# Soft MoE weights split to halves in other phases, and in other pieces and queues

## What is computed

```python
x = x + tanh(g_xattn[0]) * L0_xattn(ctx, ctx, layernorm(x), ssm_kernel, D)   # causal convolution of products of 8 x 8 heads
x = x + tanh(g_ffn[0])   * L0_ffn(layernorm(x), ...)                         # 8 experts, top 2, and a shared expert
x = x + tanh(g_xattn[1]) * L1_xattn(layernorm(x), ctx, Wq, Wg, bg, Wkv, Wo)  # linear attention
x = x + tanh(g_ffn[1])   * L1_ffn(layernorm(x), gamma, beta, mu, scale, W1, b1, W2, b2)   # Soft MoE
```

```python
x_n = l2norm(x_ln) * scale;  mu_n = l2norm(mu, axis=0)
logits = einsum('bnd,des->bnes', x_n, mu_n)
dispatch, combine = softmax over tokens, softmax over all slots
slot_in = einsum('bnd,bnes->besd', x_ln, dispatch)
h = gelu(slot_in @ W1[e] + b1[e]);  slot_out = h @ W2[e] + b2[e]
out = einsum('bsd,bns->bnd', slot_out, combine)
```

## Time and profile before

| | us |
|---|---|
| median of 3 runs | 1921.96 (1918.27 to 1922.52) |
| the profiled execution | 1921.54 |
| span of its profile | 1919.8 |
| PE busy / DVE / ACT / POOL | 1594.0 / 1134.1 / 735.5 / 480.1 |

### The profile page before, as it was taken

The page is one execution under the profiler, slowest core; times in us unless marked ns, Lnnn a source line. Parts: engine busy times, 40 slices in busy tenths (PEclk is TensorE's granted clock), DMA queues, the critical chain, the costliest instruction groups (busy, mean ns, idle before and its releaser), DMA issues. The chain is left out here.

```text
span 1919.8 us, 27754 instructions
## 1 busy us (share of the span) xinstructions
PE 1594.0 (83%) x9596; PEld 927.9 (48%) x9596; DVE 1134.1 (59%) x2222; ACT 735.5 (38%) x1380; POOL 480.1 (25%) x368
## 2 busy tenths in 40 slices
PE   2978874899926988985879887586999999999997
PEld 2767762344413555552435444243555555555554
DVE  4978864555362222225768685566667676676664
ACT  2322112334321222213423332165656566565552
POOL 1334330444342433323232321134020110201000
PEclk9999996999967999996999999798999999999999
DMA  8323334333346555635330300643415143151432
GB/s 184 82 84 106 126 108 140 115 114 127 104 142 132 123 150 146 152 107 197 99 110 12 100 3 20 234 134 83 86 42 116 33 87 81 44 115 33 77 73 49
DMA packets 261179, 195.26 MB, mean 102 GB/s; under 512 B 183426, under 2 KB 212098, under 8 KB 259410
## 3 DMA queue, kind: packets, MB, share of 16 engines
q1 hardware_dynamic: 253920, 174.03, 33.6%
q0 software_dynamic: 5680, 18.62, 3.5%
q10 hardware_dynamic: 1474, 1.21, 0.3%
HBM read 110.37 MB, written 39.67 MB: 78 GB/s over the span
## 5 line engine op out<-in xcount | busy, mean ns | idle before, releaser
L1958 POOL TENSOR_TENSOR s_h_lo<-s_h,s_h_hi 128x512 f16<-128x512 f32 x32 | 37.0, 1155 | 515.9 <-DVE s_h_hi L2176 515.9
L1180 DVE TENSOR_TENSOR e_h<-e_up,e_silu 128x352 f32<-128x352 f32 x39 | 20.5, 525 | 177.7 <-ACT e_silu L1142 177.7
L507 PE MATMUL ring<-prod_hi,toep 128*128 128x288 f16 x320 | 92.8, 290 | 32.6 <-DVE terms L427 21.6
L2194 PE MATMUL s_ring<-w_mu,s_xt_hi 128*128 128x512 f16 x256 | 98.4, 384 | 15.1 <-DVE s_xt_lo L2095 14.7
L306 POOL TENSOR_TENSOR prod_lo<-prod,prod_hi 128x2304 f16<-128x2304 f32 x16 | 73.3, 4581 | 102.5 <-ACT prod_hi L343 97.8
L2195 PE MATMUL s_ring<-w_mu,s_xt_hi 128*128 128x512 f16 x256 | 98.1, 383 | 0.0
L2196 PE MATMUL s_ring<-w_mu,s_xt_lo 128*128 128x512 f16 x256 | 98.0, 383 | 0.0
L2100 DVE TENSOR_REDUCE s_top<-s_lg 128x1 f32<-128x512 f32 x64 | 43.9, 686 | 90.5 <-ACT s_lg L2004 90.3
L2194 PE MATMUL s_acc<-w_w_hi,s_g_hi 128*128 128x512 f16 x256 | 97.1, 379 | 0.2
L2194 PE MATMUL s_ring<-w_w,s_xt_hi 128*128 128x512 f16 x256 | 97.0, 379 | 0.0
L2195 PE MATMUL s_ring<-w_w,s_xt_hi 128*128 128x512 f16 x256 | 97.0, 379 | 0.0
(11 more groups left out here) (386 smaller groups left out, 4750.4 us busy)
## 6 DMA issues: line engine op xcount, KB each, us to landing
expert_rows<-e_y SPq DMA_DIRECT2D x39, 256.0 KB, 2.3
toep<-ssm_split SPq DMA_DIRECT2D x14, 512.0 KB, 5.8
stage<-in_L_ffn_gate_w SPq DMA_DIRECT2D x8, 704.0 KB
stage<-in_L_ffn_up_w SPq DMA_DIRECT2D x8, 704.0 KB
c_rows<-in_ctx SPq DMA_DIRECT2D x8, 512.0 KB, 10.2
x_rows<-in_x SPq DMA_DIRECT2D x8, 512.0 KB
res<-in_x SPq DMA_DIRECT2D x128, 32.0 KB
w_in<-in_L_ffn_W SPq DMA_DIRECT2D x16, 256.0 KB, 5.2
```

The lines of the kernel that those rows point to most:

```text
L507: nc.tensor.matmul(out, w_hi, hi, start=(n == 0), stop=False)
L2194: mm(out_, a[0], b_[0], start=first, stop=False)
```

## The change

- **Convolution.** W1 and W2 are both split there: 32 pieces (`part_in`, `part_q`, three buffers as before), two in each step on ACT and on POOL. The pieces of W2 are written to a new tensor `w2_split` in the device's memory. SP stores and reloads the pieces ahead of the step's row stores; the residual rows from the third step's on are loaded by ACT, eight transfers at the end of a step's body.
- **Experts.** `mu` goes in pieces of 256 KB, 16 loads and 16 stores, one of each with a tile; the parts of a quarter are shifted (`quarter_at`, a quarter every 8 tiles from tile 4), each engine at its own distance; the store of a tile's result is issued five tiles behind instead of three.
- **Soft MoE.** The operations `Q` are gone; W2's halves are loaded from `w2_split`, four transfers of 1 MB behind W1's. `E(3)` moves up before the last `Z`, and `E(4)` to `E(7)` of the first batch come after its first GELU in a list of their own (`body0`).

The diff, cut to its core:

```diff
@@ conv_stage
+        def load_res(eng, s):
+            for j in range(SSM_I):
+                eng.dma_start(res[j * 16:j * 16 + 16, s % 2, :], x_s[s, j]).then_inc(res_loaded[s % 2], 16)
...
+            def load_part(n):
+                v = n % PART_BUFS
+                if n < STEPS:
+                    sp.dma_start(part_in[:, v, :].rearrange("p (e h) -> p e h", e=JE), w1_d[n // KD, n % KD]).then_inc(part_loaded[v], 16)
+                else:
+                    sp.dma_start(part_in[:, v, :], w2[n - STEPS]).then_inc(part_loaded[v], 16)
...
             for s in range(STEPS):
                 if s + T_BUFS < STEPS:
                     load_toeplitz(s + T_BUFS)
                 if s == 0:
-                    for v in range(W1_BUFS):
-                        load_w1(v)
+                    for n in range(PART_BUFS):
+                        load_part(n)
+                for n in (2 * s, 2 * s + 1):
+                    store_part(n)
+                    if n + PART_BUFS < 2 * STEPS:
+                        load_part(n + PART_BUFS)
                 store(s)
-                if s + 2 < STEPS:
-                    load_res(s + 2)
-                if s >= 2:
-                    store_w1(s - 2)
-                    if s - 2 + W1_BUFS < STEPS:
-                        load_w1(s - 2 + W1_BUFS)
...
@@ conv_stage, gpsimd
                 if s >= 2:
-                    rest_of_w1(s - 2)
+                    rest_of_parts(s - 2)
@@ conv_stage, scalar
                 if s + 2 < STEPS:
                     split(s + 2)
-                split_w1(s)
+                split_parts(s)
+                if s >= 1 and s + 1 < STEPS:
+                    act.wait_ge(added, s)
+                    load_res(act, s + 1)
@@ expert_phase
-        PEEL, SPAN = 9, 9
+        PEEL, FIRST, PERIOD = 9, 4, 8
...
+        def quarter_at(n, part):
+            j, rest = divmod(n - FIRST - part, PERIOD)
+            return j if not rest and 0 <= j < NJ else None
...
@@ expert_phase, sync
+            LAG = 5
...
+            def background(n):
+                if 1 <= n <= 2 * KD:
+                    load_mu(*divmod(n - 1, KD))
+                for j, c in ((quarter_at(n, 13 + c), c) for c in range(KD)):
+                    if j is not None:
+                        store_mu(j, c)
+                        if j + 2 < NJ:
+                            load_mu(j + 2, c)
...
-                if n >= 3:
-                    store(n - 3)
...
+                if n >= LAG:
+                    store(n - LAG)
+                background(n)
@@ soft_moe_phase
-                  + softmax_in(2) + w2_split(0, 2) + E(0) + late("Z", 4) + softmax_in(3) + w2_split(2, 4) + E(1) + late("Z", 5) + softmax_in(4)
-                  + w2_split(4, 6) + E(2) + late("Z", 6) + softmax_in(5) + w2_split(6, 8) + late("Z", 7) + softmax_in(6) + softmax_in(7) + softmax_in(8)
-                  + w2_split(8, 10) + softmax_in(9) + E(3) + w2_split(10, 12) + softmax_in(10) + E(4) + w2_split(12, 14) + E(5) + w2_split(14, 16)
-                  + E(6) + E(7))
+                  + softmax_in(2) + E(0) + late("Z", 4) + softmax_in(3) + E(1) + late("Z", 5) + softmax_in(4)
+                  + E(2) + late("Z", 6) + softmax_in(5) + E(3) + late("Z", 7) + softmax_in(6) + softmax_in(7) + softmax_in(8) + softmax_in(9) + softmax_in(10))
...
+        body0 = []
+        for op in body:
+            body0 += [op]
+            if op == (0, "HG", 0):
+                body0 += E0(4) + E0(5) + E0(6) + E0(7)
...
+            for j in range(NJ):
+                sp.dma_start(w.w2[:, j].rearrange("p q e d -> p (q e d)"), w2_split[j]).then_inc(w2_in[j], 16)
```

More of the change, by code:

```diff
@@ L259, in _ @@
                     load(t, 0, u)
-            load_res(0)
-            load_res(1)
+            for s in range(2):
+                load_res(sp, s)
             for u in range(2):
@@ L1068, in _ @@
                                              ).then_inc(gathered[n % U], 16)
-                if n >= U and n - U < NJ * SPAN:
-                    quarter(*divmod(n - U, SPAN))
+                background(n)
+            for n in range(TILES, FIRST + PERIOD * (NJ - 1) + 16):
+                background(n)
         @block.tensor
@@ L1115, in step, with background @@
                     last.then_inc(contracted, 1)
-            def quarter(j, part):
-                if part == 2:
+            def background(n):
+                j = quarter_at(n, 4)
+                if j is not None:
                     pe.wait_ge(MU["ones"], 1)
@@ L1124, in quarter @@
                     last.then_inc(MU["summed"], 1)
-                if part == 4:
+                j = quarter_at(n, 6)
+                if j is not None:
                     pe.wait_ge(MU["inverted"], j + 1)
@@ L1163, in quarter @@
                     nc.scalar.activation(mu_scale[:, :], mu_ps[:, :], ACT.Copy).then_inc(MU["scale"], 1)
-                if part in (6, 7):
-                    if part == 6:
-                        act.wait_ge(MU["stored"], j * 16)
-                    for c in range((part - 6) * 2, (part - 6) * 2 + 2):
+                for j, c in ((quarter_at(n, 9 + c // 2), c) for c in range(KD)):
+                    if j is not None:
+                        if not c:
+                            act.wait_ge(MU["stored"], j * KD * 16)
                         act.wait_ge(MU["scaled"], j * KD + c + 1)
                         nc.scalar.activation(mu_q[:, 0, c, :], mu_in[:, j % 2, c, :], ACT.Copy).then_inc(MU["hi"], 1)
-            over_tiles(step, quarter)
+            over_tiles(step, background)
         @block.vector
@@ L1193, in step, with background @@
                     nc.vector.tensor_copy(y[:, u, :], out_ps[:, b, :]).then_inc(y_done, 1)
-            def quarter(j, part):
-                if part == 3:
+            def background(n):
+                j = quarter_at(n, 5)
+                if j is not None:
                     inv = mu_inv[:, j, :]
```

187 lines of the change are left out of this document (77 added, 110 removed).

## The result

| | before | after |
|---|---|---|
| median of the runs, us | 1920.12 (4 runs) | 1902.13 (1901.38 to 1905.24, 4 runs) |
| the profiled execution | 1921.54 | 1905.24 |
| its span | 1919.8 | 1903.5 |
| mean granted clock | 0.939 | 0.936 |

The ratio is 0.9913, with a 95% interval of 0.9888 to 0.9938: 18 us faster. The forecast was 1869 us, with a range from 1853 to 1889; the time lies outside it. Two of the three parts brought what was worked out for them, and the third, the convolution, lost where it should have gained.

The account below looks back on a forecast made before the run. The prediction took SP's late issuing to bind the convolution, and PE's waits for transposed rows to cost the experts. Gains of 23, 24 and 6 us (convolution, experts, Soft MoE) made 53 us: 1869 us, range 1853 to 1889.

Parts of the forecast that it names:

- the loop over two steps: Convolution: stores, SP's issuing and landing take 27.0 us, 13.5 a step; with less issuing 20.4 us, no longer binding.
- The nine waits: Convolution: PE's once-a-step waits of 19.4 us in all shrink to 0.2 us each, gaining 17.6 us.
- PE's own work: Convolution: PE's step without its wait of 2.2 us is 11.3 us; the forecast took 11.5 us a step.
- ACT's put wait: Convolution: PE's 3.39 us wait for ACT, held behind a late piece of W1, goes away, gaining 3.4 us.
- Steps 2 and 3: Convolution: the second POOL piece falls into the normalisation, where PE waits for DVE, costing 1.5 us.
- The tail: End of the convolution: row stores, not stores of W1's halves, are SP's last issues and end earlier, gaining 3.5 us.
- Rival 3: Convolution: ACT becomes the bound if an issue there costs about 1.6 us instead of 0.65; slower, chance 0.04.
- rival 1: Convolution: the DVE-POOL lock becomes the bound, each `pairs` waiting out two pieces; 7 us gained, 1880 us, chance 0.18.
- Rival 5: Convolution: SP's lateness is not the cause, so only experts and Soft MoE gain; 1892 us, chance 0.05.
- Experts: Experts: PE's waits for transposed rows mostly go and the clock rises; 24.0 us gained in sum.
- rival 2: Experts: small `mu` pieces cost as much as large ones, so the gain is 8 us, not 24; 1885 us, chance 0.08.
- Soft MoE: Soft MoE: less work on ACT and POOL brings `G` 8.1 us earlier, less 2 for the clock; 6 us gained.

Follow-up runs that it names:

- e3: The kernel after with the residual row loads back on SP's queue behind the row stores: 1903.3 us.
- e4: The kernel after with each residual load of 16 rows cut into two of 8 rows: 1868.2 us.
- e2: The kernel before with only the residual row loads moved from SP's queue to ACT's: 1937.2 us.
- e5: The kernel before with residual loads on ACT's queue and each cut into two of 8 rows: 1912.6 us.
- e1: The kernel before with only the experts' part of the change: 1895.8 us.
- e10: The kernel after with the four pairs E(4) to E(7) put back ahead of the second batch's X in the Soft MoE: 1905.6 us.
- e7: The kernel after, storing the rows of steps 0 to 13 a second time from ACT's queue in eight 32 KB transfers of 16 rows a step: 1960.4 us.

## Why the prediction was wrong

**The step that failed** is the loop over two steps of the convolution, "9.0 us to the stores, 11.5 us of issuing, 6.5 us to land". It closed to 27.0 us by the numbers, and two steps took 27.0, so I took the 6.5 us of landing for a constant and the issuing for what binds. The landing time was itself a queue behind the row transfers on two engines. When the issuing was shortened, the landing rose from 6.2 to 13.0 us. The agreement of the sum was no evidence: any loop that waits for itself closes. The DMA share of 0.37 in the earlier trace rows looked far from full; it is a mean over 16 engines, of which two had no gap: there were never fewer than two packets in flight.

Term by term:
- *The nine waits, +17.6 us.* They lost 8 us instead, 1.0 us a step. Two busy engines, with 32 KB more in each step, ask for 1.3. W2's pieces, which the prediction costed at nothing for DMA, are by that count what loads them, though no run has them alone; moving the residual rows relieves nothing, as e3 shows.
- *PE's own work, 11.3 us a step.* Right: 11.28 us in e4's shortest steps. The 11.5 us a step of the forecast was met within 0.3 us in e4 (11.8), once the rows had more engines.
- *ACT's put wait, +3.4.* It is gone, and step 5 starts 0.3 us earlier than in before (132.99, 133.25). Steps 5 and 6 then lose 3.0 us, and step 7 starts at 162.51 instead of 159.73.
- *Steps 2 and 3, -1.5.* They take 42.6 us instead of 39.4. In e4, which has the cut, it is 42.6 too, so the two engines are not the cause; nor is the second piece shown to be, since e2, which has one piece a step, takes 42.3. This stays open.
- *The tail, +3.5.* From the start of step 15 to `x_in` it is 28.2 us instead of 27.3. ACT waits 8.54 and 5.94 us there for the last pieces of W2, and the last row stores go out behind them:

```profile
280.00 0.63 ACT L352 ACTIVATE part_q<-part_in 128x512 f16<-128x512 f32 x1 [8.54 <-DMA part_in<-in_L_ffn_W]
...
291.89 0.63 ACT L352 ACTIVATE part_q<-part_in 128x512 f16<-128x512 f32 x1 [5.94 <-DMA part_in<-in_L_ffn_W]
...
295.09 4.97 SPq L245 DMA_DIRECT2D after_conv<-gated  x8
306.50 0.38 SPq L617 DMA_DIRECT2D x_in<-after_conv  x1
```

- *ACT's issues.* 0.64 us each, eight in 5.1 us, as SP's row had said. Rival 3, the slower one, was priced on the wrong thing: in e2 the move alone is slower by 17 us, at near this price of an issue (5.6 to 6.2 us for eight), and VectorE waits for loads that ACT reaches late.
- *The lock, rival 1.* It is real, but did not arise: in after `pairs` takes 2.29 and 0.42 us in the mean from 157 to 265 us, and does not meet the pieces. In e5 it costs VectorE 1.8 us a step.
- *Rival 5* came nearest: the moved work does not shorten what binds. It stood at 1892 us with a chance of 0.05, and it still had the convolution at no change. Its chance rested on the closed loop, and was too small.
- *Experts, +24.0.* 24 us by e1's median, 27 in the profile. Of PE's waits for `e_xt` only the first, 13.4 us at the phase's start, is left, and before has it too (13.1, ahead of the window of the earlier trace rows). That the small pieces would cost as much (rival 2) did not come: 256 KB pieces are no worse here than 1 MB ones, although the rule of the Trainium skill (DMA: Bandwidth & Descriptors, section "Bandwidth") that the prediction named asks for 1 MiB or more. How the gain divides was wrong: rival 2 is what happens at a store distance of 3, and at 5 it is covered, for 17.5 to 21 us and not 10. That leaves 3 to 10 us to the pieces, not the 12.3 of the two long waits.
- *Soft MoE, +6.* 5.4 us. `G` comes 91.2 us into the phase instead of 99.7, 8.5 us earlier (8.1 forecast), behind a wait of 8.18 us (6). e10 confirms that the order of the pairs is not what gave it. That leaves W2's halves, gone from ACT and POOL, which no run has alone.

The range failed as well. The lower bounds that the prediction gave its terms add up to 17 us (convolution 5 + 0 - 2.3 + 2.2, experts 12 + 0 - 1.5, Soft MoE 2), not to the 35 from which it drew its edge of 1887; the measured 18 us lie there.

With e4's cut the whole change gives 1868.2 us, near the 1869 that was forecast. That is no merit of the forecast, since without the cut its condition failed, and it is luck in part: e4's profile gains 15.4 us in the convolution, 27.5 in the experts and 7.6 in the Soft MoE, where 23, 24 and 6 were forecast.

## What to carry to other kernels

Before a transfer's issue time is taken for a bound, ask what its landing time consists of: divide the bytes by engines, not by 16, and look for a floor in the slices of the DMA view, since a low mean share can hide two engines without a gap. The number of engines comes from the shape of a transfer's access pattern; where its slowest dimension is 2, cutting the transfer so that it is 8, at twice the issues, paid 34 us here. And a loop whose parts add up to the period that was measured proves nothing on which of the parts would shrink.

## What was unexpected of the hardware

- Transfers of 16 rows from a pattern of [2][8][512] move at 50 GB/s together, at a DMA share of 0.13, on SP's queue as on ACT's; in 8 rows each they no longer bound a step.
- In e2, where two queues start such transfers at the same moment, mostly 28 to 47 GB/s moved in place of 50; in after and e7 two queues with rows under way moved 49 to 50. Why e2 is different is open.
- Loads moved to another engine's queue are issued when that engine gets to them in its own order. ACT reached the residual loads of e2 behind a late piece of W1, and VectorE waited for them before every addition, 22.8 us in eight steps and 12.34 us before the last.
- The same convolution code had a granted clock of 1.00 and of 0.92 in two profiled executions, and took 294.9 and 302.1 us.
